# Attention by pairs of heads: TensorE transposes before it scores, ScalarE copies before its exponents

## The reference

```
L0: q,k,v = rms_norm(x) @ (v_qkv | l_qkv by token type); rotary on q,k
    x += causal_softmax(q k^T / sqrt(32)) v @ dense            # 112 x 112 scores per head   ("self")
    x += softmax(cq(x) ck^T) cv @ cdense                       # 375 keys, 16 heads of 16    ("cross0")
    x += (silu(h @ gate) * (h @ up)) @ down
L1: q = layernorm(x) @ Wq; k,v = ctx @ Wkv                     # 375 keys, 16 heads of 64    ("cross1")
    x += tanh(g) * softmax(where(mask, q k^T / 8, min)) v @ Wo
    x += tanh(g) * gelu(layernorm(x) @ W1) @ W2
L2: mp = ctx @ W_mem^T; m = softmax(x mp^T / sqrt(512)) mp     # 375 keys, one head          ("memory")
    x = rms_norm(x + sigmoid([x, m] @ W_gate + b) * m)
L3: as L1, with weights of its own                             #                             ("cross3")
```

## Time and profile before

| | before |
|---|---|
| median of 3 runs | 2151.87 us |
| profiled execution / its span | 2153.12 us / 2151.3 us |
| TensorE matmul busy | 1999.6 us (93%) |
| VectorE busy | 1179.8 us (55%) |
| ScalarE busy | 852.6 us (40%) |
| chain that ended last, TensorE's share | 81% |
| granted TensorE clock, mean | 0.954 |

### The profile page before, as it was taken

One profiled execution on the slowest core, in us unless ns is written; L12 is line 12 of the kernel. 1 busy time (PEld: TensorE's weight loads), 2 busy tenths in 40 slices (PEclk: granted clock), 3 DMA queues, 4 the chain that ended last, 5 costly groups with the idle time before them and its releaser, 6 DMA issues.

```text
span 2151.3 us, 35629 instructions
## 1 busy us (share of the span) xinstructions
PE 1999.6 (93%) x12588; PEld 1694.3 (79%) x12588; DVE 1179.8 (55%) x3046; ACT 852.6 (40%) x2198; POOL 887.9 (41%) x1037
## 2 busy tenths in 40 slices
PE   4999897988889999999999999998878999998998
PEld 3865586766679999888888887996547888887898
DVE  6778766566555245354666645422165666664422
ACT  2026525565422112125666633322234666661321
POOL 3340302114048899974121126881043121103785
PEclk9999698897789999999999999999999999999999
DMA  3110100001013333331000022332131000001232
GB/s 120 40 55 2 45 8 15 9 21 50 3 43 105 117 108 114 122 103 36 14 20 12 12 83 69 108 108 75 67 102 42 9 18 12 22 2 40 88 109 83
DMA packets 38191, 118.87 MB, mean 55 GB/s; under 512 B 6169, under 2 KB 10265, under 8 KB 38017
## 3 DMA queue, kind: packets, MB, share of 16 engines
q1 hardware_dynamic: 31408, 107.92, 16.2%
q10 hardware_dynamic: 6608, 8.68, 1.4%
HBM read 114.75 MB, written 1.84 MB: 54 GB/s over the span
## 4 chain that ended last, share of the span: by engine, by line
PE 81%; DVE 9%; POOL 5%; issue 2%; ACT 2%; DMA 1%; DVEq 0%; SPq 0%; ACTq 0%; POOLq 0%
PE psum L544 15%; PE psum L545 13%; PE psum L546 13%; PE psum L755 8%; PE psum L766 7%; PE psum L809 6%; PE psum L537 4%; PE psum L660 4%; PE psum L662 4%; PE psum L661 4%; POOL wl L1603 3%; DVE rstd L1196 1%; DVE xc L1211 1%; POOL wh L1595 1%; PE psum L823 1%
## 5 line engine op out<-in xcount | busy, mean ns | idle before, releaser
L1603 POOL TENSOR_TENSOR wl<-raw,wh 128x256 fp32r<-128x256 f32 x656 | 517.7, 821 | 13.7
L1595 POOL TENSOR_SCALAR wh<-raw 128x1024 fp32r<-128x1024 f32 x164 | 183.7, 1120 | 459.5 <-PE psum L546 205.2
L544 PE MATMUL psum<-nh,wh 128*128 128x448 f32 x904 | 347.2, 384 | 14.5 <-DVEq L1379 7.8
L545 PE MATMUL psum<-nl,wh 128*128 128x448 f32 x904 | 336.9, 373 | 0.0
L546 PE MATMUL psum<-nh,wl 128*128 128x448 f32 x904 | 336.0, 372 | 0.0
L988 ACT ACTIVATE probs_t<-masked_t,nmin 112x375 f32<-112x375 f32 (+1 forms) x384 | 207.2, 540 | 129.8 <-DVE nmin L1314 113.3
L766 PE MATMUL psum<-cst,probs_t 112*125 112x112 f32 (+1 forms) x1304 | 240.5, 291 | 16.3 <-DVE probs_t L1325 16.2
L766 PEld LDWEIGHTS psum<-cst,probs_t 112*125 112x125 f32 (+1 forms) x1304 | 196.3, 194 | 59.0 <-DVE probs_t L1325 25.4
L1325 DVE TENSOR_SCALAR probs_t<-probs_t,rinv 112x376 f32<-112x376 f32 (+1 forms) x520 | 218.0, 419 | 18.5
L1451 DVE TENSOR_TENSOR hid_l<-scr,hid_h 128x448 fp32r<-128x448 f32 x108 | 94.1, 871 | 229.0 <-ACT hid_h L1063 228.4
L1314 DVE CUSTOM_DVE_ANT_0 masked_t<-psum,maskf 112x375 f32<-112x375 f32 x256 | 139.3, 545 | 124.4 <-PE psum L755 123.9
(11 more groups left out here) (178 smaller groups left out, 3854.8 us busy)
## 6 DMA issues: line engine op xcount, KB each, us to landing
raw<-in_walls SPq DMA_DIRECT2D x183, 512.0 KB, 3.5
raw<-in_ctxF SPq DMA_DIRECT2D x24, 375.0 KB, 3.0
ctxb<-in_ctxF ACTq DMA_DIRECT2D x8, 375.0 KB, 3.8
ctxt<-in_ctxK ACTq DMA_DIRECT2D x8, 375.0 KB
x<-in_xT ACTq DMA_DIRECT2D x2, 896.0 KB, 11.6
outT<-x SPq DMA_DIRECT2D x2, 896.0 KB, 5.8
mask<-in_kmask ACTq DMA_DIRECT2D x16, 41.0 KB, 2.6
vself<-in_tt SPq DMA_DIRECT2D x1, 448.0 KB, 6.8
```

Source lines behind the costliest of these rows:

```text
L544: nc.tensor.matmul(out, ah, bh, start=(i == 0), stop=False)
L545: nc.tensor.matmul(out, ah, bl, start=False, stop=False)
L1595: nc.gpsimd.tensor_scalar(high, src, 1.0, 1.0, ALU.mult, ALU.mult).then_inc(split_h, 1)
L1603: last = nc.gpsimd.tensor_tensor(low[cut], src[cut], high[cut].bitcast(F32), ALU.subtract)
```

## The change

Heads are handled two by two (`pair`) on all engines; the memory attention keeps one head for each step. With n the number of a pair:

- TensorE, in step n: value sums, the transposes of both heads of pair n-2, then the scores of pair n, then all projections of its two heads (`finish`). In memory the scores stand first.
- ScalarE: the copies of pair n-2 first, then both exponents of pair n, then its share of the projections.
- VectorE: both smallest values of pair n, one reciprocal for both heads of pair n-1, both scalings, its share of the projections of pair n-1, then the sums of the group that ends with pair n-4.
- cross0 uses the masking instruction with a mask of zeros, so its exponent reads SBUF and TensorE waits for VectorE, not for ScalarE, before it scores again.
- 6 rows of probabilities and 4 of masked scores. The latter lie where the norms keep scratch.
- In cross1 and cross3 the two parts of V stand at the second and third of each four heads, with no part made ahead of the attention.

```diff
--- before.py
+++ after.py
@@ -55,7 +55,8 @@
 RING = 4
 BIG = 3.4028234663852886e38
 LAG = 2
-NPROB = 3
+NPROB = 6
+NMASK = 4
 NTURN = 5
 POOL = 3
 
@@ -286,14 +288,15 @@
         rinv = sb("rinv", [S, NPROB])
         eps = sb("eps", [P, 2])
         o_a = place[0]
-        masked_t = sb("masked_t", [S, 2, S2])
+        masked_t = at("masked_t", [S, NMASK, S2], F32, o_s + 2 * 4 * 8 * S)
+        assert 2 * 4 * 8 * S + 4 * NMASK * S2 <= o_n - o_s
         probs_t = sb("probs_t", [S, NPROB, 376])
         hid_h = at("hid_h", [P, 2, HALF], F32R, o_a)
         hid_l = at("hid_l", [P, 2, HALF], F32R, o_a + 8 * HALF)
         vtmp = at("vtmp", [S, 2, D], F32, o_s)
         assert place[0] <= 229344, place[0]
         vS = vself[0:S, :].rearrange("p (b d) -> p b d", b=B)
-        masked_s = [masked_t[:, i, :] for i in range(2)]
+        masked_s = [masked_t[:, i, :] for i in range(NMASK)]
         probs = [probs_t[:, i, :] for i in range(NPROB)]
         probsT = [probsT_t[:, i, :] for i in range(NTURN)]
 
@@ -498,10 +501,10 @@
 
             if not a.k_heads:
                 return []
-            first = {att_c0: -4}.get(a, -1)
-            second = {att_c0: -1}.get(a, 1)
+            first = {att_c0: -4}.get(a, 1)
+            second = {att_c0: -1}.get(a, 2)
             if s == -1:
-                return [("K", i, 0) for i in range(a.k_slots - 1)] + [("V", 0, 0)] + ([("V", 0, 1)] if second < 0 else [])
+                return [("K", i, 0) for i in range(a.k_slots - 1)] + ([("V", 0, 0), ("V", 0, 1)] if second < 0 else [])
             out = []
             if s % a.k_heads == 0:
                 out.append(("K", s // a.k_heads + a.k_slots - 1, 0))
@@ -737,7 +740,7 @@
                     return
                 if s >= 2:
 
-                    pe.wait_ge(a.maxed if a.mask else a.exped, s)
+                    pe.wait_ge(a.maxed, s)
                 wide = a.nk + a.nk % 2
                 passes = [(0, 0), (0, 1), (1, 0)] if a.k_heads else [(0, 0)]
                 for n, (i, j) in enumerate(passes):
@@ -829,20 +832,31 @@
                         for c in (2 * e, 2 * e + 1):
                             chunk_last[(0, "v", c)] = (tile_ready, plan.n)
 
+            def finish(a, n):
+                pairs, wide = a.steps // a.pair, a.quad // a.pair
+                w = n - LAG - 1
+                if 0 <= w < pairs and w % wide == wide - 1:
+                    weigh(a, w // wide)
+                if 0 <= n - LAG < pairs:
+                    for s in range(a.pair * (n - LAG), a.pair * (n - LAG + 1)):
+                        turn(a, s)
             def attention(a):
-                for s in range(a.steps + LAG + 2):
-                    if s < a.steps:
...
-                        weigh(a, w // a.quad)
+                pairs = a.steps // a.pair
+                for n in range(pairs + LAG + 2):
+                    heads = range(a.pair * n, a.pair * n + a.pair)
+                    if a is not att_2:
+                        finish(a, n)
+                    if n < pairs:
+                        scores(a, heads[0])
+                        for s in heads:
+                            for unit in projected(a, s):
+                                project(a, *unit)
+                            if a is att_self and s % 2 == 0 and s // NH + 1 < B:
+                                values(s // NH + 1, s % NH // 8, s % 8 // 2)
+                    if a is att_2:
+                        finish(a, n)
 
             pe.wait_ge(cst_in, 16)
 
@@ -978,16 +992,36 @@
                 dst = v1[0:KEYS, i % 2, 2 * part:2 * part + (2, 1)[part], :]
                 nc.scalar.copy(dst.rearrange("p c n -> p (c n)"), bank[0:KEYS, 0:w]).then_inc(emptied["act"], 1)
 
+            def copies(a, n):
+                for t in range(a.pair * (n - LAG), a.pair * (n - LAG + 1)):
+                    if t < 0 or t % a.group < a.group - 1:
+                        continue
+                    g = t // a.group
+                    act.wait_ge(a.turned, t + 1)
+                    if g >= NTURN:
+                        act.wait_ge(a.summed, (g - NTURN) * a.group // a.quad + 1)
+                    w = max(a.group, a.chunks) * S
+                    nc.scalar.copy(probsT[g % NTURN][0:a.kw, 0:w], t_bank(g)[0:a.kw, 0:w]).then_inc(a.probs_out, 1)
+                    if a is att_2 and 3 <= g < B - 1:
+                        act.wait_ge(a.summed, g - 2)
+                        key_major(g + 1)
             def attention(a):
-                for s in range(a.steps + LAG):
-                    if s < a.steps:
+                pairs = a.steps // a.pair
+                for n in range(pairs + LAG):
+                    heads = range(a.pair * n, a.pair * n + a.pair)
+                    if a is not att_2:
+                        copies(a, n)
+                    for s in heads if n < pairs else ():
                         act.wait_ge(a.maxed, s + 1)
                         if s >= NPROB:
                             act.wait_ge(a.turned, s - NPROB + 1)
-                        src = masked_s[s % 2][:, 0:a.nk] if a.mask else s_bank(s)[:, 0:a.nk]
+                        src = s_bank(s)[:, 0:a.nk] if a is att_2 else masked_s[s % NMASK][:, 0:a.nk]
                         nc.scalar.activation(probs[s % NPROB][:, 0:a.nk], src, ACT.Exp, scale=-1.0,
                                              bias=nmin[:, s % NPROB:s % NPROB + 1],
                                              accum_out=rsum[:, s % NPROB:s % NPROB + 1]).then_inc(a.exped, 1)
+                    for s in heads if n < pairs else ():
                         for unit in projected(a, s):
                             project(a, *unit)
                         if a is att_self and s % 8 == 7 and s // NH + 1 < B:
@@ -996,17 +1030,8 @@
                             context(a, s // NH + 2)
                         if a is att_2 and s + 2 < B:
                             context(a, s + 2)
-                    t = s - LAG
-                    if t >= 0 and t % a.group == a.group - 1:
...
-                            key_major(g + 1)
+                    if a is att_2:
+                        copies(a, n)
 
             def key_major(b):
                 act.dma_start(ctxt[0:KEYS, b % 4, :], ctxK[b]).then_inc(ctxt_in[b % 4], 16)
@@ -1290,49 +1315,57 @@
                 nc.vector.scalar_tensor_tensor(vS[:, b, :], bank[0:S, :], vmT[:, 1, b:b + 1], vtmp[:, b % 2, :],
                                                ALU.mult, ALU.add).then_inc(emptied["dve"], 1)
 
+            def smallest(a, s):
+                b, h = s // a.nh, s % a.nh
+                col = nmin[:, s % NPROB:s % NPROB + 1]
+                dve.wait_ge(a.scored, s + 1)
+                if s >= NMASK:
+                    dve.wait_ge(a.exped, s - NMASK + 1)
+                if a is att_2:
+                    nc.vector.tensor_reduce(col, s_bank(s)[:, 0:a.nk], AX_X, ALU.min).then_inc(a.maxed, 1)
+                    return
+                if a.mask == "keys" and h == 0:
+                    dve.wait_ge(a.mask_in[b % 2], 16 * (b // 2 + 1))
+                    nc.vector.tensor_scalar(maskf[:, b % 2, :], mask8[:, b % 2, :], -BIG, BIG,
+                                            ALU.mult, ALU.add).then_inc(a.masked, 1)
+                    dve.wait_ge(a.masked, b + 1)
+                m = {"causal": causal, "keys": maskf[:, b % 2, :], None: maskf[:, 0, :]}[a.mask]
+                nc.vector.tensor_tensor_reduce(out=masked_s[s % NMASK][:, 0:a.nk], in0=s_bank(s)[:, 0:a.nk],
+                                               in1=m, scale=1.0, scalar=BIG, op0=ALU.add, op1=ALU.min,
+                                               accum_out=col).then_inc(a.maxed, 1)
             def attention(a):
                 if a.nk == S2:
 
                     dve.wait_ge(chain, link(nc.vector.memset(probs_t[:, :, S2:S2 + 1], 0.0)))
-                wide = a.nk + a.nk % 2
-                for s in range(a.steps + LAG + 2):
...
-                        dve.wait_ge(a.recip, r + 1)
+                if a is att_c0:
+                    dve.wait_ge(chain, link(nc.vector.memset(maskf[:, 0, :], 0.0)))
+                pairs, wide = a.steps // a.pair, a.nk + a.nk % 2
+                for n in range(pairs + LAG + 3):
+                    if n < pairs:
+                        for s in range(a.pair * n, a.pair * n + a.pair):
+                            smallest(a, s)
+                    late = range(a.pair * (n - 1), a.pair * n) if 0 < n <= pairs else ()
+                    if late:
+                        own = slice(late[0] % NPROB, late[0] % NPROB + a.pair)
+                        dve.wait_ge(a.exped, late[-1] + 1)
+                        nc.vector.reciprocal(rinv[:, own], rsum[:, own]).then_inc(a.recip, 1)
+                        dve.wait_ge(a.recip, n)
+                    for r in late:
                         pr = probs[r % NPROB][:, 0:wide]
                         nc.vector.tensor_scalar(pr, pr, rinv[:, r % NPROB:r % NPROB + 1], None, ALU.mult)\
```

(12 more changed lines are left out.)

42 lines of the change are left out of this document (1 added, 41 removed).

## The result

| | before | after |
|---|---|---|
| median | 2150.11 us (4 runs, 2148.07 to 2154.09) | 2514.84 us (4 runs, 2510.39 to 2519.45) |
| ratio | | 1.1694, 95% interval 1.1663 to 1.1725: slower |
| profiled execution / its span | 2153.12 / 2151.3 us | 2512.07 / 2510.3 us |
| TensorE / VectorE / ScalarE busy | 1999.6 / 1179.8 / 852.6 us | 2129.6 / 1138.6 / 865.1 us |
| clock, mean | 0.954 | 0.909 |

The account below looks back on a forecast made before the run. It took cross1 and cross3 as full on TensorE, cross0 as idling for ScalarE's exponent. Added waits 196 + 40 + 8, clock 66, small terms 12 + 6 made +328 us: 2481 profiled, 2480 median, range 2330 to 2630.

Parts of the forecast that it names:

- First wait, the pool: cross1 and cross3: V waits until VectorE empties the previous pair's K tile, 1.6 us of TensorE idle in each pair.
- The masking step: VectorE in cross1: time from one masking to the next, between 0.47 and 0.62 us, taken as 0.50.
- the clock term: All attentions: emptier TensorE spends more time at the lower clock, +66 us in sum (0 to +240).
- The clock's 17 us in cross1: cross1 and cross3: half the cost of a quarter of the time at the lower clock, +17 us a stage.
- Second and third wait, self: Self: transposes wait for VectorE's scaling, value sums for its sums' copies; 1.93 and 2.99 us a pair, +40 us taken.
- a quarter of the time is +24: cross0: a quarter of the time at the lower clock, about 6 us a pair against 4.04, adds 24 us.
- 12 us to longer ends of the stages: Ends of each stage: a lag of two pairs and a VectorE step delays each by some 3 us, +12.
- The 6 us for the keys' mask: VectorE's path: 16 keys' mask operations of about 0.4 us now lie on it, +6 us.
- Rival 2: Only the pool's wait is real; new buffers hide the loop in self and cross0: 2317 us; 0.18 together with Rival 4.
- Rival 3: VectorE empties K and scales before TensorE asks, cross0 wins 56 us: faster, about 2097 us; chance 0.04.
- Rival 4: Waits overlap each other and low-clock stretches, each about half its size: 2336 us; 0.18 together with Rival 2.
- Rival 1: The clock falls deeper, half the time at the lower level in the attentions: 2645 us; chance 0.15.

Follow-up runs that it names:

- k_emptied_first: The changed kernel, but VectorE does its share of the projections of pair n-1 ahead of the maskings of pair n, in all attentions: 2363.63 us.
- v_ahead_of_k: The changed kernel, but in cross1 and cross3 TensorE projects a pair's V part ahead of its K tile, and ScalarE copies in that order: 2431.01 us.
- the filler: The changed kernel with 10 thrown-away TensorE matmuls of 376 columns ahead of each second value sums in cross0: 2468.89 us.
- k_and_sums_first: The changed kernel, but VectorE copies a group's sums and does its projections of pair n-1 ahead of the maskings of pair n: 2166.64 us.
- all_orders: The changed kernel, but TensorE scores first, ScalarE copies behind its exponents, VectorE copies sums and empties the K tile ahead of its maskings: 2096.97 us.
- copies_behind: The changed kernel, but ScalarE copies pair n-2 behind the exponents and projections of pair n, no longer ahead of them: 2852.65 us.

## Why the prediction was right

2480 us were forecast, 2514.84 measured: +328 us against +359 in the profiled executions. By its steps:

- **First wait, the pool.** V 3.25 us after the scores, seen 3.28; four heads 11.81, seen 11.80. The masking step, of which no row had told more than a range, is 0.47 where I took 0.50, and from the emptied K tile to V it is 0.15 (1391.94 to 1392.09) where I took 0.07; the two nearly cancel. TensorE's matmuls idled 87.8 us in 61 waits, 1.44 each, where 1.6 was forecast, and its busy share in cross1 is 77%, near 75% as forecast. k_emptied_first and v_ahead_of_k show the cause. With the clock term 115 us a stage were expected, 112.2 and 114.1 came.
- **The clock's 17 us in cross1: the size came out, the cause only in part.** The clock there fell only to 0.97. From 1124.87 to 1485.04 us, 29 periods of four heads took 12.42 us on average, 18 us more in all than 29 times 11.80. Of these, 13 pairs of scalings beside GpSimd (below) make 5.8 us, which the prediction had no term for, and seven mask operations of 0.35 us on VectorE's path 2.5. So little more than half is left for the clock.
- **Second and third wait, self.** 1.93 and 2.99 us were expected, 1.84 (194.26 to 196.10) and 2.83 (191.43 to 194.26) seen at full clock: four heads 4.67 and not 4.92 us. 48 us with the clock's part, 51.2 came, and that is in part luck: 32 times 4.67 - 3.37 is 42 and not 50 us, which I had cut to 40 for another reason, and I gave the clock only 8 although it fell from 0.88 to 0.68.
- **cross0: the mechanism right, the clock's term mis-sized.** 3.33 us a pair expected, 3.24 to 3.28 seen in the shortest. The stage was to grow by 32 us and grew by 65.4. The step that was too small is "a quarter of the time is +24". With a clock of 0.70 the share of time at the lower level is (1 - 0.70) / 0.5 = 60%; even the 0.82 of the earlier trace rows stands for 36%, so a quarter was less than the kernel before had, although the change makes the stage emptier. By the pairs: the 14 with a wait for the sums' bank took 115.3 us where 6.20 each make 86.8, and the other 49 took 191.1 where 3.33 each make 163.2. That the clock is at work in this the filler shows. The waits alone and my +24 gave 283 us, 24 under the 307.2 seen; the other 9 us of the miss are in the base, 254 less 3 us of window against 241.8 from first to last scores.
- **The rest.** The prediction gave 12 us to longer ends of the stages, and 16.1 came outside the windows, but not where it had put them. Around self and cross0 nothing was added (0.3 us at most), 13.6 us lie between the last scores of cross1 and the first of cross3, a stretch that holds an MLP and the memory attention, and 2.4 behind cross3. Over the changed kernel and its variants, the time outside the windows is 1258.6 to 1265.1 us where VectorE copies the sums last, and 1241.5 to 1252.5 where it copies them first; before had 1244.0. So the order of VectorE's copies is likely to be at work there too; which operation waits I have not followed. The 6 us for the keys' mask lie within cross1 and cross3 and are counted above.
- **Rivals.** Rival 2 falls with the stage table (self and cross0 grew), and its 56 us for cross0, like those of rival 3, were more than the 32.5 us that TensorE idled there. Rival 3, the faster side, was decided as it said: VectorE's chain is 3.28 us and TensorE asks at 1.65. With VectorE's steps alone in another order (k_and_sums_first) the kernel comes back to 2166.64 us and isn't faster; with TensorE's and ScalarE's too (all_orders) it is 2096.97. Rival 4 falls with the 11.80 us of four heads: the pool's wait came in full. Rival 1, half of the time at the lower clock, was right of the clock in cross0 (0.70) and in self (0.68) and wrong in cross1 and cross3. Its +58 for cross0 doesn't follow from its own 4.8 us a pair: 64 pairs are 307 us, +48 over 259, and 307.2 were measured.
- **ScalarE.** The prediction gave its new order no term, and in the sum that was right; but copies_behind shows that I had not understood why: its place is held by TensorE's order.

## What to carry to other kernels

When engines are given new orders together, write down for each of them what stands between a step and its release on the next engine; a wait in a ring of tiles is set by the neighbour in the ring, and one short operation on another engine, five places too late, cost 150 us here. Release what others wait for (a tile, a bank) at the head of a step and do the new work behind it, if it is ready by then: ScalarE's copies at the head of its step cost 194 us where TensorE's transposes come last in theirs. Such waits hide each other: take them away together, since one alone shows too little. And a wait on TensorE can cost more than its length where the clock already swings: removing 41 us of it in cross0 gave 69, though in self 34 expected gave 34.
